# Mixer of a Mamba block: D*u scaled by ScalarE and added through transposes, in place of matmuls by a diagonal

## What is computed

```python
u = jax.nn.silu(jnp.transpose(xc, (0, 2, 1)))      # xc: causal conv of the projected input
...                                                 # B, C and dt are projections of u
def step(h, inp):
    dt_t, B_t, C_t, u_t = inp
    dA = jnp.exp(dt_t[..., None] * A)
    h = dA * h + (dt_t * u_t)[..., None] * B_t[:, None, :]
    y = jnp.einsum('bdn,bn->bd', h, C_t)
    return (h, y)
...
y = jnp.swapaxes(ys, 0, 1) + u * D
y = y * jax.nn.silu(z)
return y @ out_proj_w.T
```

## Time and profile before

| | |
|---|---|
| median of 3 runs | 3674.62 us (3673.96 to 3679.95) |
| span of the profiled execution | 3674.1 us, 0.5 us under that median; its own time outside the span isn't shown |
| busy: PE, DVE, ACT, POOL | 3352.4, 3256.0, 2759.3, 2577.3 us |
| mixer | from the first scan at 71 us to about 2690 us: 16 chunks of some 164 us |

### The profile page before, as it was taken

How to read it: one execution, slowest core, us unless ns; L and a number is a source line. 1 busy time by engine, 2 the same in 40 slices (tenths; PEclk the granted TensorE clock), 3 DMA queues, 4 the chain that set the end, 5 groups by cost and what they waited for, 6 DMA issues and landing times. The chain is left out here.

```text
span 3674.1 us, 50128 instructions
## 1 busy us (share of the span) xinstructions
PE 3352.4 (91%) x16962; PEld 2370.5 (65%) x16962; DVE 3256.0 (89%) x3376; ACT 2759.3 (75%) x5350; POOL 2577.3 (70%) x2045
## 2 busy tenths in 40 slices
PE   6989989899999989899989989898889998889997
PEld 3666666666666666666666666666657776557776
DVE  3999999999999999999999999999967887876886
ACT  5888797888789788977978787888655554875553
POOL 3898988989898988989898988989921111551100
PEclk7999999999999999999999999999999999999998
DMA  3020211202020211202020210202111113641212
GB/s 134 10 92 19 92 38 65 85 18 85 19 92 19 92 47 55 84 18 85 19 98 23 83 69 33 84 19 85 63 58 35 53 53 143 236 184 40 70 36 87
DMA packets 83586, 249.89 MB, mean 68 GB/s; under 512 B 15212, under 2 KB 24044, under 8 KB 73092
## 3 DMA queue, kind: packets, MB, share of 16 engines
q1 hardware_dynamic: 82564, 245.65, 18.6%
q10 hardware_dynamic: 768, 1.05, 0.1%
HBM read 204.73 MB, written 41.95 MB: 67 GB/s over the span
## 5 line engine op out<-in xcount | busy, mean ns | idle before, releaser
L956 POOL TENSOR_TENSOR slot<-dtu,b_rep 128x512 f32<-128x512 f32 x960 | 1206.4, 1277 | 78.5 <-PE ysum L454 77.8
L966 POOL TENSOR_TENSOR slot<-slot,c_rep 128x512 f32<-128x512 f32 x768 | 974.1, 1278 | 157.3 <-ACT carry L763 92.5
L454 PE MATMUL ysum<-ident,slot 128*128 128x128 f32 x6144 | 831.4, 280 | 31.9 <-POOL slot L966 16.7
L454 PEld LDWEIGHTS ysum<-ident,slot 128*128 128x128 f32 x6144 | 725.9, 145 | 173.0 <-issue 103.1
L754 ACT ACTIVATE state<-dt,aneg 128x512 f32<-128x512 f32 x960 | 655.4, 688 | 237.9 <-DVE slot L1065 200.8
L1065 DVE TENSOR_TENSOR slot<-state,c_rep 128x512 f32<-128x512 f32 x768 | 514.3, 672 | 0.0
L572 PEld LDWEIGHTS state<-diag_b,dtu_t 128*128 128x128 f32 x3072 | 385.0, 194 | 130.3 <-issue 121.1
L572 PE MATMUL state<-diag_b,dtu_t 128*128 128x128 f32 x3072 | 422.7, 281 | 33.0 <-ACT carry L763 16.6
L745 ACT ACTIVATE slot<-dt,aneg 128x512 f32<-128x512 f32 x576 | 405.4, 711 | 23.1 <-PE ysum L454 23.0
L1057 DVE TENSOR_TENSOR_SCAN slot<-state,slot 128x512 f32<-128x512 f32 x288 | 343.3, 1209 | 44.1 <-ACT state L754 33.6
L1057 DVE TENSOR_TENSOR_SCAN slot<-state,carry,slot 128x512 f32<-128x512 f32 x288 | 360.6, 1269 | 6.3 <-POOL slot L956 3.3
(11 more groups left out here) (272 smaller groups left out, 6291.9 us busy)
## 6 DMA issues: line engine op xcount, KB each, us to landing
c_rep<-rows_of_b_and_c SPq DMA_DIRECT2D x64, 1024.0 KB, 5.1
xres_l<-between_layers SPq DMA_DIRECT2D x18, 1536.0 KB, 9.8
xn_l<-between_layers SPq DMA_DIRECT2D x13, 1536.0 KB, 7.1
b_rep<-rows_of_b_and_c SPq DMA_DIRECT2D x16, 1024.0 KB, 4.5
between_layers<-y SPq DMA_DIRECT2D x10, 1536.0 KB, 6.4
xn<-in_x SPq DMA_DIRECT2D x16, 768.0 KB, 4.5
b_rep<-rows_of_b_and_c SPq DMA_DIRECT2D x16, 768.0 KB, 4.1
xres<-in_x SPq DMA_DIRECT2D x16, 768.0 KB, 4.5
```

Source lines behind the costliest of these rows:

```text
L454: last = mm(ysum[:, cols], slot[:, (NS * k + n) % SLOTS, cols], ident[:], start=first and j == 0, stop=final, is_transpose=True, skip_grou ...
L956: tt(slot[:, q % SLOTS], dtu[:, k % 2], b_rep[:, b_row(n)], ALU.mult).then_inc(dbu_done, 1)
L966: tt(slot[:, q % SLOTS], slot[:, q % SLOTS], c_rep[:, n], ALU.mult).then_inc(pool_mult_done, 1)
```

## The change

D*u is no longer a matmul. ScalarE copies u with D as its scale, one value per partition, into a new tile `skip` of two buffers (`skip_u`), at the steps of SKIP_AT: 93 (for k = 0 of the next chunk), 10, 24, 42, 54 and 72; for the first chunk just ahead of its scan. TensorE adds `skip` to `ysum` by four transposes (`turn_skip`), like a 17th product, ahead of the first sum of each k. turn_y keeps its transposes alone. `diag_d`, its six VectorE instructions and the semaphore diag_set go. The loads of B are issued in runs of equal distance (`b_runs`); for the states that GpSimd drives here a group of four gives one run, the same transfer as before.

```diff
+SKIP_AT = (93, 10, 24, 42, 54, 72)
...
-        diag_d = sb("diag_d", [P, KT, P])
+        skip = sb("skip", [P, 2, T])
...
+            def turn_skip(c, k):
+                if later(KT * c + k):
+                    pe.wait_ge(yt_copied, KT * c + k)
+                pe.wait_ge(skip_done, KT * c + k + 1)
+                for j in range(T // P):
+                    cols = slice(j * P, (j + 1) * P)
+                    last = mm(ysum[:, cols], skip[:, k % 2, cols], ident[:], start=j == 0, stop=False, is_transpose=True,
+                              skip_group_check=True)
+                last.then_inc(skip_turned, 1)
...
             def sum_state(c, k, n):
                 first, final = by_sum(n, n) == 1, by_sum(n, n) == NS
-                if first and later(KT * c + k):
-                    pe.wait_ge(yt_copied, KT * c + k)
+                if first:
+                    turn_skip(c, k)
...
-                mm(y[:], diag_d[:, k], u[h][:, k], start=True, stop=False, skip_group_check=True)
                 pe.wait_ge(yt_copied, KT * c + k + 1)
                 for j in range(T // P):
                     cols = slice(j * P, (j + 1) * P)
-                    last = mm(y[:, cols], yt[:, cols], ident[:], start=False, stop=True, is_transpose=True,
-                              skip_group_check=True)
+                    last = mm(y[:, cols], yt[:, cols], ident[:], start=True, stop=True, is_transpose=True)
...
+            def skip_u(c, h, k):
+                act.wait_ge(u_done, KT * c + k + 1)
+                if later(KT * c + k, 1):
+                    act.wait_ge(skip_turned, KT * c + k - 1)
+                af(skip[:, k % 2], u[h][:, k], ACT.Copy, scale=dskip[:, k:k + 1]).then_inc(skip_done, 1)
...
+                    for k in range(KT):
+                        if q == SKIP_AT[k] and (after or k > 0):
+                            skip_u(c if k > 0 else d, h if k > 0 else 1 - h, k)
...
             copy_u(0, 0)
+            skip_u(0, 0, 0)
             scan(0, 0, False, True)
...
-            dve.wait_ge(consts, 1)
-            for k in range(KT):
-                v.tensor_scalar(diag_d[:, k], ident[:], dskip[:, k:k + 1], None, ALU.mult).then_inc(diag_set, 1)
```

26 lines of the change are left out of this document (18 added, 8 removed).

## The result

The changed kernel takes **3696.47 us** (median of 4 runs, 3694.33 to 3697.75) against 3675.80 for the kernel before (4 runs, 3673.96 to 3679.95): ratio 1.0051, 95% interval 1.0036 to 1.0065. It is slower by about 20 us, outside the range of the prediction. The profiled execution before (span 3674.1 us) is at the lower end of these.

The account below looks back on a forecast made before the run. The limit goes from engine to engine, TensorE bounding a chunk's first third. Odd chunks -2.5, even chunks +1.0, setup +0.6 sum to -0.9 us on 3674.1, given as 3673.7 us against a median of 3674.62 (no change); range 3661 to 3687.

Parts of the forecast that it names:

- TensorE's longer waits cost nothing: Savings at steps 29, 38, 73 and 81 only lengthen TensorE's waits for VectorE's conv or ScalarE: nothing.
- The first third: Steps 1 to 30, TensorE never idle: 0.86 us goes at step 1, 0.44 comes at steps 4 and 20; net +0.02.
- ScalarE's copies: 96 more activations, 0.61 us each behind another, 3.7 us a chunk; hidden in waits except at step 54 of even chunks.
- The recovery at step 69: Even chunks: step 54's 0.61 us delay is regained at step 69, TensorE being 0.86 - 0.61 = 0.25 us early; GpSimd keeps +0.11.
- Rival B: ScalarE becomes the bound at steps 54 and 72 of even chunks: 2 x 0.61 x 8 = 10 us, 3684; chance 0.14.
- The gain in odd chunks: Step 56's saved matmul starts GpSimd earlier, shortening VectorE's wait at step 74: -0.36 us in each of 7, -2.5 us.
- Setup: The first copy stands between L774 and the first decay, for which VectorE waits: +0.6 us.
- TensorE's clock: Wait for the conv grows from 1.77 to about 2.2 us; granted clock may fall there, 1.7 us each time; chance 0.07.
- Rival C: TensorE's clock falls at the conv wait: 13 us, 3687, if in half of 15 chunks; 3699 in all; chance 0.07.
- the things that would show me wrong: Even chunks longer than 164.6 us, the clock dropping at the conv wait, or the first third getting shorter.

Follow-up runs that it names:

- e1: The kernel before with ScalarE's 96 scaled copies of u added, their result unused, D*u still a matmul: 3687.4 us.
- e11: The changed kernel with two matmuls put back as work without use, at steps 38 and 56: 3695.2 us.
- e5: The changed kernel with one matmul put back as work without use, at step 38: 3691.9 us.
- e2: The changed kernel without ScalarE's copies; TensorE adds u itself, unscaled, by the transposes: 3684.9 us.
- e3: The changed kernel with the copies of k = 3, 4, 5 at steps 28, 42, 78 instead of 42, 54, 72: above the expected 3675 to 3682 us.
- e4: The changed kernel with two useless 128x512 matmuls put back per chunk, at steps 38 and 68: 3688.7 us.
- e10: The changed kernel with copies at steps 36, 42 and 78, tile 1's transposes of D*u at step 31, no useless matmul: 3679.1 us.
- e9: The changed kernel with moved copies, tile 1's transposes of D*u at step 31 and one useless matmul, at step 38: 3675.3 us.
- e6: The changed kernel with one useless 128x512 matmul added at step 68, nothing at step 38: 3698.6 us.

## Where the prediction held and where it failed

The forecast was -0.9 us and the profile shows +20.5. Three steps failed: that TensorE's longer waits cost nothing (10.7 us of clock falls), that the 0.61 us of step 54 is made good at step 69, and that odd chunks gain 0.36 us. The last two and the first third make the small losses of 6.0 us, where the forecast for all chunks was -1.5.

**The first third** (net +0.02): nearly. The terms were -0.86, +0.44, +0.44; measured +0.13 in even chunks and +0.21 in odd ones. The first is the mis-sized one. At step 1 the diagonal's matmul started 0.89 us behind the drive in front of it (1223.62, the drive at 1222.73), and the transposes that now stand there start later than that:

```profile
1231.93 1.05 PE L593 MATMUL state<-diag_b,dtu_t 128*128 128x128 f32 x8
1233.00 0.63 PE L535 MATMUL pz<-ident,yt 128*128 128x128 f32 x4
```

That is 1.07 us, a gap that the matmul had covered, so 0.68 us are saved in this chunk (0.66 to 0.74 at step 4) instead of 0.86. What they wait for, the trace doesn't say. VectorE's wait at step 3 went from 1.03 to 0.31 us, and then those at step 11 (1.64 to 2.08) and step 27 (0.44 to 0.88) grew: -0.72 + 0.44 + 0.44 = +0.16 in chunk 8. I had expected shorter waits at steps 7 (0.99, as before) and 11 as well, as if the lead of step 3 could be gained three times, and the loss at the layer norm (0.49, as before). The even chunks of 164.1 us that I named don't follow from my own +0.13 either, which gives 164.4.

**ScalarE's copies**: right in price. Timeline of ScalarE, even chunk 8, step 54, and the group over the mixer (columns of the earlier trace rows):

```profile
1486.29 0.71 ACT L801 ACTIVATE skip<-u,dskip 128x512 f32<-128x512 f32 x1
1486.91 0.57 ACT L714 ACTIVATE acc<-pz,halo_bias,cw 128x1 f32<-128x1 f32 x2
```

```profile
L801 ACT ACTIVATE skip<-u,dskip 128x512 f32<-128x512 f32 x96 | 68.0, 709 | 0.0
```

One takes 709 ns and moves what is behind it by 0.62 us (forecast 0.61). The Trainium skill, page "ScalarE: Activation LUTs", section "What ACT_TABLE_LOAD costs", gives 705 and 612 ns by an estimate, and the trace agrees. Its 93 ns for the pointer operand don't make the whole difference of the two rows, as I had written: 711 less 583 is 128 ns. In odd chunks the copies are hidden, as forecast (e1: 163.84 for 163.91). ScalarE's waits for VectorE at that line, forecast 50 us shorter in total, are 23.5 shorter; the trace doesn't divide the rest.

```profile
ACT state L775 <- DVE slot L1096: 129.2, 118, 2.7
```

**The recovery at step 69** (0.61 at step 54, of which 0.11 was to last): wrong, and the largest of the small terms: 0.5 us a chunk in 8 chunks, 4 us. I subtracted 0.61 from 0.86 as if both ran on TensorE. But the drive at step 58 waits for a carry, that is for VectorE, which is the late one; e11 shows that the 0.86 us count for 0.1. Since the loss lasts to the end, this is **Rival B's** mechanism at half of its size: +0.64, not 2 x 0.61, since the copy at step 72 adds nothing lasting by itself (even chunks without a fall are +0.61 at step 53 and +0.6 at the end in e1).

**The gain in odd chunks** (-0.36 at step 74, 2.5 us in all): wrong by the same error. GpSimd's run did start on an earlier sum, but the next sum stood behind a dt_proj that waits for VectorE, and 0.57 of 0.63 us were given back within 5 us. Odd chunks are 0.22 us longer in place of 0.34 shorter.

**Setup** (+0.6): VectorE's wait ahead of the first scan is 24.14 us for 23.53, which fits. But e5, with the same copy in its setup, has its first scan at 71.24 us, 0.16 before the kernel without the copy, so the term is smaller than the spread and its being right is not shown.

```profile
72.29 3.45 DVE L1088 TENSOR_TENSOR_SCAN slot<-state,slot 128x512 f32<-128x512 f32 x3 [24.14 <-ACT state L775]
```

**TensorE's clock** (Rival C, 0.07): this is half of the result, and it was given far too small a chance. The wait at step 39 went to 2.18 us (forecast 2.2), the clock fell there in 3 of 7 odd chunks, and each cost 1.4 us (forecast 1.7). I had dismissed it because the first third, full of transposes, holds the full clock; but that stretch has no idle time, so it says nothing about transposes followed by a wait. And I weighed one wait only. The one at step 70, 1.80 us before, was another of that length, put at nothing with the rest. The change touched it from both sides: four transposes added ahead of it shorten it by 0.44 us (1.36 in e2 and e3), and ScalarE's copy at step 72 makes it 0.6 longer, together 1.97. The Trainium skill, page "TensorE: Matmul & The Clock Gate", section "Part 4: PE-mode transpose", says that transposes don't engage the full clock as matmuls do. No run here needs this: at step 70, e2 and e3 have the transposes and a short wait and no falls, and e1 the old matmuls and a long wait and falls, and the first third, at 1.00 with many transposes among its matmuls, keeps the clock without idle time. At step 39, where the matmul just ahead went and the wait grew together, it is not excluded. Why one wait of 2.18 us ends in a fall and the next doesn't stays open.

Of the things that would show me wrong, two came about: even chunks above 164.6 us, and a falling clock at the conv wait.

## What to carry to other kernels

A saving on an engine counts up to its next wait, not to the end: before setting it against a loss elsewhere, find the first instruction behind it that waits for another engine (here a carry and a bank, 1 to 3 us later), and ask whether that engine is the late one. Where the granted clock already falls at some waits of a kernel, list every wait of TensorE of about the same length, and price a change that lengthens one at the fall's full cost, here 1.3 to 1.4 us a time where work that others wait for stands right behind, and nothing where another wait takes it up. Work added for another engine goes to a place behind which its engine waits anyway, and work that can be done at any time goes out of the stretch in which its engine is never idle: here 0.44 us cost all of it at step 20 and, at step 31, nothing in odd chunks and 0.16 us in even ones.

## What the hardware did that I had not expected

- TensorE did more and the kernel got faster: two useless 128x512 matmuls a chunk (0.86 us each) took 8 us off the changed kernel (e4, 3688.7 for 3696.5; ratios 1.0028 and 1.0051), and leaving one out cost 3.9 us (e10 against e9).
- The granted clock falls to 0.50 (for 3.4 us at 1522.20) behind some waits and not others of the same length: 2.18 us at step 39 ended in a fall in chunk 11 and in none in chunk 7 of one execution. At step 70, 1.80 us kept the clock in six chunks of six; 1.97 us, with four transposes more ahead, lost it in five of seven, and 2.41 to 2.61 us, with the matmul work of before, in four of five.
- How many of equal waits end in a fall isn't fixed: five kernels with the same 2.18 us at step 39 have 3, 4, 4, 4 and 5 falls in seven chunks (after, e2, e3, e10, e6).
- Four transposes directly behind a group of drives started 1.07 us behind that group's start, where a 128x512 matmul had started after 0.89 us. The 0.18 us between were not in the matmul's price.
